# Causal mask of the M scores: from a VectorE add to a TensorE product with the identity

## What is computed

```python
scores = jnp.einsum('bhqd,bhkd->bhqk', q, k) / np.sqrt(HEAD_DIM)
causal = jnp.tril(jnp.ones((t, t), dtype=bool))
scores = jnp.where(causal, scores, -jnp.inf)
attn = jax.nn.softmax(scores, axis=-1)
out = jnp.einsum('bhqk,bhkd->bhqd', attn, v)
```

## Time and profile before

| what | us |
|---|---|
| median of 3 runs | 2979.12 |
| lowest and highest of them | 2971.29, 2981.47 |
| the profiled execution | 2984.29 |
| its span, first to last instruction | 2982.5 |
| mean granted TensorE clock in it | 0.98 of full |

### The profile page before, as it was taken

How to read it: one execution, slowest core, us unless ns; L and a number is a source line. 1 busy time by engine, 2 the same in 40 slices (tenths; PEclk the granted TensorE clock), 3 DMA queues, 4 the chain that set the end, 5 groups by cost and what they waited for, 6 DMA issues and landing times.

```text
span 2982.5 us, 116966 instructions
## 1 busy us (share of the span) xinstructions
PE 2787.7 (93%) x49280; PEld 1459.4 (49%) x49280; DVE 2351.8 (79%) x5811; ACT 1748.6 (59%) x3425; POOL 1038.6 (35%) x2006
## 2 busy tenths in 40 slices
PE   4979999999999999999999999999999999999978
PEld 1345454645545455454645545454454545545442
DVE  4768788797887978889797887979788797887835
ACT  1725656566565665656566565666656566565734
POOL 4243432334343333432334342233433333343110
PEclk7999999999999999999999999999999999999987
DMA  3010101101010010101101010110101001010000
GB/s 115 6 54 23 54 23 31 34 24 54 24 46 19 23 58 24 55 23 32 34 23 54 27 50 12 38 44 23 54 24 39 26 23 57 25 54 19 8 23 5
DMA packets 117452, 103.30 MB, mean 35 GB/s; under 512 B 19990, under 2 KB 116160, under 8 KB 116672
## 3 DMA queue, kind: packets, MB, share of 16 engines
q1 hardware_dynamic: 116928, 95.83, 10.5%
HBM read 8.56 MB, written 4.19 MB: 4 GB/s over the span
## 4 chain that ended last, share of the span: by engine, by line
PE 73%; DVE 19%; issue 4%; ACT 3%; POOL 1%; SPq 0%; DMA 0%; ACTq 0%; DVEq 0%; POOLq 0%
PE bank L526 52%; PE pv L644 17%; DVE mx L844 9%; PE bank L532 2%; PE bank L654 1%; DVE hid L949 1%; DVE hid L955 1%; DVE xn L741 1%; ACT hid L1078 1%; DVE bn L726 1%; DVE bank L849 1%; DVE latn L741 1%; ACT probs L1045 1%; DVE factored L741 1%; DVE l1bn L726 0%
## 5 line engine op out<-in xcount | busy, mean ns | idle before, releaser
L1045 ACT ACTIVATE probs<-bank 128x512 f32<-128x512 f32 x2688 | 1479.3, 597 | 855.6 <-PE bank L526 849.3
L844 DVE TENSOR_REDUCE mx<-bank 128x1 f32<-128x512 f32 x2048 | 1282.2, 682 | 81.4 <-PE bank L526 71.4
L849 DVE CUSTOM_DVE_ANT_0 bank<-bank,mask 128x128 f32<-128x128 f32 (+3 forms) x1024 | 480.4, 515 | 97.8 <-PE bank L526 97.6
L1192 POOL TENSOR_SCALAR_AFFINE_SELECT probs<-probs 128x256 f32<-128x256 f32 (+1 forms) x640 | 230.1, 362 | 765.8 <-ACT probs L1045 759.1
L526 PE MATMUL bank<-kp_B,qp_B 72*32 72x512 bf16 x4096 | 440.0, 394 | 28.7 <-DVE mx L844 24.5
L526 PE MATMUL bank<-kp_A,qp_A 72*32 72x512 bf16 x4096 | 403.7, 382 | 40.9 <-DVE mx L844 31.7
L526 PE MATMUL bank<-qp_B,kp_B 74*32 74x512 bf16 x4096 | 430.2, 384 | 1.4 <-ACT probs L1045 1.0
L526 PE MATMUL bank<-qp_A,kp_A 74*32 74x512 bf16 x4096 | 408.1, 382 | 0.5 <-ACT probs L1045 0.5
L526 PE MATMUL bank<-kp_M,qp_M 72*32 72x128 bf16 (+3 forms) x4096 | 332.7, 307 | 21.2 <-issue 16.0
L644 PE MATMUL pv<-probs,vv_B 128*32 128x512 f32 x2048 | 281.8, 601 | 9.3 <-ACT probs L1045 9.0
L526 PE MATMUL bank<-r2T,w1s 128*32 128x512 f32 x2048 | 281.1, 597 | 4.0 <-DVE hid L922 2.0
(11 more groups left out here) (144 smaller groups left out, 3276.8 us busy)
## 6 DMA issues: line engine op xcount, KB each, us to landing
qp_M<-parts_q SPq DMA_DIRECT2D x144, 128.0 KB
kp_M<-parts_k SPq DMA_DIRECT2D x144, 128.0 KB
qp_A<-parts_q SPq DMA_DIRECT2D x144, 128.0 KB
qp_B<-parts_q SPq DMA_DIRECT2D x144, 128.0 KB
kp_A<-parts_k SPq DMA_DIRECT2D x144, 32.0 KB
xs<-x SPq DMA_DIRECT2D x16, 256.0 KB, 3.1
out<-res SPq DMA_DIRECT2D x16, 256.0 KB, 2.2
kp_B<-parts_k SPq DMA_DIRECT2D x144, 8.0 KB
```

Source lines behind the costliest of these rows:

```text
L844: v.tensor_reduce(mx[:, g % 2, at:at + 1], s1[BANK[a, g, u]][:], AX.X, ALU.max) \
L849: v.tensor_tensor_reduce(bank[:, 0:keys], bank[:, 0:keys], mask[:, SEQ - keys:SEQ], 1.0, LOWEST, ALU.add, ALU.max, mx[:, g % 2, at:at + 1] ...
L1045: act.activation(probs[:, slot, :], s2[BANK2[a, g, u]][:], ACT.Exp).then_inc(sig[f"{a}_exp"], 1)
L1192: pool.affine_select(out=v, in_=v, compare_op=ALU.is_ge, fill=0.0, base=0, pattern=pattern, channel_multiplier=-1).then_inc(sig["M_masked" ...
```

## The change

PE adds the mask. After the four matmuls of an M unit, which no longer close their accumulation, four more follow into the unit's last 128 columns: the identity (`identb`, 128 x 128, bf16, already there) is the stationary operand, and `maskb` (128 x 128, bf16, -1e30 above the diagonal) the moving one. The semaphore for DVE is raised by the last of these. DVE takes a plain `tensor_reduce` of the unit's width for all three attentions. POOL builds `maskb` in place of the wider `mask`.

```diff
-        mask = sb("mask", [P, SEQ])
+        maskb = sb("maskb", [P, P], BF16)
@@ TensorE, score_max
-                in_columns(s1[BANK[a, g, u]][:, 0:keys], q_rows(a, h, ROWS1)[:, P * t:P * t + P],
-                           k_rows(a, h, ROWS1)[:, 0:keys]).then_inc(sig[f"{a}_s1_ps"], 1)
+                bank_of = s1[BANK[a, g, u]]
+                ins = in_columns(bank_of[:, 0:keys], q_rows(a, h, ROWS1)[:, P * t:P * t + P],
+                                 k_rows(a, h, ROWS1)[:, 0:keys], True, a != "M")
+                if a == "M":
+                    ins = in_columns(bank_of[:, P * t:P * t + P], identb[:], maskb[:], False, True)
+                ins.then_inc(sig[f"{a}_s1_ps"], 1)
@@ VectorE, score_max
-                if a != "M":
-                    v.wait_ge(sig[f"{a}_s1_ps"], total(b, f"{a}_s1_ps", n + 1))
-                    v.tensor_reduce(mx[:, g % 2, at:at + 1], s1[BANK[a, g, u]][:], AX.X, ALU.max) \
-                        .then_inc(sig[f"{a}_s1_read"], 1)
-                else:
-                    v.wait_ge(sig["M_s1_ps"], total(b, "M_s1_ps", n + 1))
-                    keys, bank = P * (t + 1), s1[BANK[a, g, u]]
-                    v.tensor_tensor_reduce(bank[:, 0:keys], bank[:, 0:keys], mask[:, SEQ - keys:SEQ], 1.0, LOWEST,
-                                           ALU.add, ALU.max, mx[:, g % 2, at:at + 1]).then_inc(sig["M_s1_read"], 1)
+                keys = P * (t + 1) if a == "M" else SEQ
+                v.wait_ge(sig[f"{a}_s1_ps"], total(b, f"{a}_s1_ps", n + 1))
+                v.tensor_reduce(mx[:, g % 2, at:at + 1], s1[BANK[a, g, u]][:, 0:keys], AX.X, ALU.max) \
+                    .then_inc(sig[f"{a}_s1_read"], 1)
@@ GpSimd, setup
-            link(pool.memset(mask[:], 0.0))
-
-            link(pool.affine_select(out=mask[:, SEQ - P:SEQ], in_=mask[:, SEQ - P:SEQ], compare_op=ALU.is_ge,
-                                    fill=MASKED, base=0, pattern=[[-1, P]], channel_multiplier=1))
+            link(pool.memset(maskb[:], 0.0))
+            link(pool.affine_select(out=maskb[:], in_=maskb[:], compare_op=ALU.is_ge, fill=MASKED, base=0,
+                                    pattern=[[-1, P]], channel_multiplier=1))
```

More of the change, by code:

```diff
@@ L62 @@
 KCH = {"M": D, "A": KV0 * HD, "B": HD}
-LOWEST = -3.0e38
 MASKED = -1.0e30
```

## The result

| | before | changed |
|---|---|---|
| median, us | 2979.30 | 3055.65 |
| lowest to highest, 4 runs each | 2971.29 to 2981.47 | 3049.12 to 3057.70 |
| profiled execution, us | 2984.29 | 3049.12 |
| its mean granted TensorE clock | 0.980 | 0.971 |

The changed kernel is slower by a ratio of 1.0258, 95% interval 1.0233 to 1.0282. I had forecast 3025 us with a range up to 3053, and the result lies 3 us above that range. The direction was right, the size was not: +76 us where the sum gave +46. The profiled execution is the fastest of the four, +65 us over that of before; the other three had a granted clock of 0.968 to 0.970.

A forecast was written before the change was run, and what follows sets the result against it. PE was taken to bound the 14 full M stages: +47.6 us there, +1.5 second stage, -2.5 first stage, -0.3 setup, together +46.3 on a median of 2979.1, giving 3025 us; range 3003 to 3053 us.

The forecast's parts named there:

- PE sets the pace in the full M stages: In 14 of 16 M stages PE is busy 60.16 of 61 us, DVE 42.42, so PE's added work counts.
- A group costs 0.057 us with its weight loads hidden: Each M unit's four added matmuls cost 0.057 us, loads keeping up: 3.65 us for a full stage's 64 units.
- Rivals 3 and 4: M-unit group costs 0.109 us like f32, 3075 us, 5%; or unhidden loads make it 0.21 us, 3165 us, 3%.
- The absorbed part: In a full M stage, added products issued ahead of PE's existing waits are free: about 0.25 us, leaving 3.4 us.
- rival 4: Weight loads of the M units' new groups not hidden: 0.21 us a group, 188 us, 3165 us in all; chance 3%.
- DVE's saving is worth nothing in the full stages: In the 14 full M stages nobody waits for DVE's maxima, so its 3.2 us a stage less work gains nought.
- Rival 1: At the A stage's start, DVE's saving shortens PE's 7.9 us of load waits: 2912 us in all; chance 5%.
- Rival 2: The cost vanishes in gaps of the M stage: at most 9 us either way, some 2979 us; chance 7%.
- The -2.5 us of the first M stage: DVE sets the pace in the first M stage, so its cheaper maxima save 2.5 us (ends 0 and -11.6).
- The setup's -0.3: POOL's smaller memset takes 0.20 us instead of 0.52, and all engines wait for this chain: -0.3 us.
- the +1.5: In the second M stage half of PE's price counts, 1.8 us, less a little of DVE's gain: +1.5 us.
- The A and B stages see no edit: No change of the A and B stages was expected, so they added nothing to the sum.

The follow-up runs named there:

- Experiments 1 and 2: Against the changed kernel: 1 keeps DVE's masked maxima beside the product, 3054.32 us; 2 leaves out the product and keeps plain maxima, 2970.70 us.
- experiment 3: Changed kernel with the mask's product issued twice in every M unit: 3090.07 us, ratio 1.0369.
- filled kernels: Kernels before, changed, plain maxima alone and half product, with unread PE products put into four waits of a period: 2970.57, 3016.12, 2968.57 and 2993.65 us.
- the misplaced one: Changed kernel with unread PE products for four waits of a period, one of them standing behind its wait instead of inside: 3046.92 us, ratio 1.0213.

## Why the prediction was right in its parts and wrong in its sum

**PE sets the pace in the full M stages: right.** Experiments 1 and 2 part the two sides: the product alone makes the stage 63.5 us, the plain maxima alone leave it at 60.3.

**A group costs 0.057 us with its weight loads hidden: right** (0.05 to 0.06 in the timeline, linear in experiment 3). Rivals 3 and 4 are out. The absorbed part was 0.5 us a stage where I took 0.25: 3.2 instead of 3.4. The rule of the Trainium skill behind rival 4 ("TensorE: Matmul & The Clock Gate", Part 3, The mechanism: a weight load overlaps with running matmuls only where the row group differs) does not hold for this pattern: the mask's operands use all 128 rows (the score products ahead of it 72, not the full rows that I wrote), and a group with its four loads passes in 0.05 to 0.06 us where the loads alone span 0.14.

**DVE's saving is worth nothing in the full stages: right.** Rival 1 is out: PE's waits for DVE at the start of the A stage are 1.11 and 0.89 us, as before. Rival 2 is out too, since the M stage grew.

**The first two M stages and the setup: not shown.** The -2.5 us of the first M stage can't be found. It took 32.1 us before, 31.5 in the changed kernel, 33.8 with the product alone and 30.2 with the plain maxima alone, which by themselves would look like gains and prices of 1 to 2 us; but it took 30.5 with the product twice, and in the filled kernels 32.1 (before), 32.7 (changed) and 32.2 (plain maxima), in one execution each. The scatter is as large as the term. The second M stage took 51.1 us before and 51.6 after, filled 51.7 and 51.6, so the +1.5 was too high. The setup's -0.3 can't be told either: the first M unit came at 52.1 and 51.1 us with the setup of before, at 48.9 to 50.7 with the changed one, and at 49.6 to 53.1 with both masks built.

**The sum of these terms: right, with some luck.** +46.3 us forecast, +45.5 measured between the filled kernels. In their profiled executions (+44.5) the part before the third M stage gives -0.8 us where the sum had -1.3, and the 14 full stages 45.3 where it had 47.6. The errors are small, but the terms of the first two stages aren't what the runs show.

**"The A and B stages see no edit": this step failed.** They see none, but they do not keep their time. I took every duration at the full clock that the windows of the kernel before showed in its steady part, and took that clock as given. But PE's waits in the A and B stages can bring it down, and it depends on the period whether they do. The kernel before has the same four waits, and in 11 of its 13 full periods they pass without effect. In the changed kernel they bring the clock down in eight of 13: 3055.65 - 3016.12 = 39.5 us in the changed kernel against 2979.3 - 2970.6 = 8.7 before, so 31 us of the 76. The profile of before held the hint, in the period from 529.6 with a clock of 0.96 and 5.8 us more than an undisturbed one. I had looked at four undisturbed periods and at the first two, and not at the rest.

The range failed with it. It held every bound of the product's price, and no term for what PE's waits do to the clock in the other stages. That it ended only 3 us short is luck: its upper end stood for weight loads that show, and they do not.

What stays open: why the waits come at a bad moment in one period and not in another. It is shown that they are the cause: filled, the effect is gone in four kernels, at the same lengths of the periods, and where one wait was left open its half clock alone stayed. How often they do it differs with the length of the undisturbed period:

| undisturbed period, us | disturbed of 13 |
|---|---|
| 177.5 (before; plain maxima alone) | 2; 1 |
| 179.0 (half of the product) | 13 |
| 180.7 (changed; product alone) | 8; 6 |
| 184.0 (product twice) | 9 |

It isn't chance within an execution, since the changed kernel and the product alone are disturbed in the same places in their first ten periods. But that the length decides is not shown: no run changed it and nothing else. The fillers were tried together only, apart from the misplaced one, so their shares are not known.

The fastest kernels are those without any product: with plain maxima and fillers 2968.6 us, with fillers alone 2970.6, with plain maxima alone 2970.7. All are faster than before by 0.3%. Of the two filled ones, timed in one series, the plain maxima lie lower (2965.9 to 2970.1 against 2969.6 to 2972.3 us), so that DVE's saving and the shorter setup may be worth 2 us; by their ratios to before the three can't be told apart. The kernels with plain maxima leave out the mask of the subtracted maximum, which may then come from a masked key, so they depend on the scores' range.

## What to carry to other kernels

Before moving work from one engine to another, ask stage by stage who sets the pace. Here the averages, 93% and 79%, named both engines, and in the edited stage one of them was busy 60 of 61 us and the other had 19 us to spare. Price an added matmul by the distance between starts of the nearest form, 0.06 us here, and not by its duration, 0.27 us; the same goes for what another engine saves. And look at the granted clock of every period, not of one: an engine that bounds the kernel and still waits 1 to 1.5 us here and there may lose its clock there as soon as anything shifts, and useless products placed inside the waits can pay for themselves.

## What the hardware showed that I had not expected

- A single wait of PE of 1.5 us, in a kernel where PE is busy for 94% of the time, was followed by a window of 10 us with a clock of 0.52. The same wait in the next period was followed by none.
- Adding PE work inside its waits made a kernel 39.5 us faster (3055.65 to 3016.12), nearly the 45.5 us that the change costs at full clock.
- Half of an added piece of work cost 53 us, all of it 76: by way of the clock, the time of this kernel isn't linear in its work, while the stage itself is (60.3, 61.8, 63.5 and 66.7 us with none, half, one and two products).
